# Three joints in blocks by halves of the tokens, and task matrices merged in two row groups between other products

## The reference

```
x = x + wide_attention(layernorm(x))             # 8 heads of 128, then @ Wout
x = x + merged_ffn(layernorm(x)):
    h = relu(x @ gate_w1.T + gate_b1);  g = mean over tokens(h @ gate_w2.T + gate_b2)    # 8 gates a batch
    mW1[b] = W1 + sum_e g[b,e] * TW1[e]          # 1024x256 for each of 16 batches
    mW2[b] = W2 + sum_e g[b,e] * TW2[e]
    out = gelu(x @ mW1[b].T + mb1) @ mW2[b].T + mb2
x = x + shared_key_attention(layernorm(x), ctx)  # L1_xattn
x = x + alibi_attention(layernorm(x))            # L1_attn
h = layernorm(x); h = h + rope_attention(rmsnorm(h)); mixture of experts       # L1_ffn
```

## Time and profile before

| | |
|---|---|
| median of 3 runs | 2373.8 us (2371.68 to 2376.3) |
| the profiled execution's own time | 2377.73 us |
| its span in the profile | 2375.9 us |
| mean granted clock of PE | 0.952 |
| busy: PE, DVE, ACT, POOL | 2179.1, 1314.4, 994.0, 332.1 us |

### The profile page before, as it was taken

How to read it: one execution, slowest core, us unless ns; L and a number is a source line. 1 busy time by engine, 2 the same in 40 slices (tenths; PEclk the granted TensorE clock), 3 DMA queues, 4 the chain that set the end, 5 groups by cost and what they waited for, 6 DMA issues and landing times. The chain is left out here.

```text
span 2375.9 us, 39783 instructions
## 1 busy us (share of the span) xinstructions
PE 2179.1 (92%) x15922; PEld 1507.1 (63%) x15922; DVE 1314.4 (55%) x2266; ACT 994.0 (42%) x1858; POOL 332.1 (14%) x366
## 2 busy tenths in 40 slices
PE   7999999999999977999998799978999998877796
PEld 4777777777777754555564677844555554545695
DVE  4556556656665634555553344347777772656554
ACT  1555555555555551343332011114666663515121
POOL 3322222222222200000000000032000000000231
PEclk9999999999999978999999899988999999898798
DMA  6877776777777521000000221123112111023312
GB/s 202 197 167 182 178 168 150 171 176 167 183 179 169 127 58 50 6 12 6 6 1 1 114 86 74 54 48 74 32 28 35 31 17 39 2 55 133 134 48 78
DMA packets 100570, 216.18 MB, mean 91 GB/s; under 512 B 58482, under 2 KB 66043, under 8 KB 94660
## 3 DMA queue, kind: packets, MB, share of 16 engines
q1 hardware_dynamic: 97652, 204.93, 34.9%
q0 software_dynamic: 2208, 6.03, 0.8%
q10 hardware_dynamic: 528, 2.69, 0.4%
HBM read 91.16 MB, written 15.20 MB: 45 GB/s over the span
## 5 line engine op out<-in xcount | busy, mean ns | idle before, releaser
L908 DVE TENSOR_REDUCE L_xattn_maxima<-L_xattn_scores 128x1 f32<-128x1024 f32 (+1 forms) x256 | 253.5, 990 | 249.2 <-PE L_xattn_scores L831 248.8
L975 ACT ACTIVATE L_xattn_probs_t<-L_xattn_turned 128x1024 f32<-128x1024 f32 (+1 forms) x256 | 220.8, 862 | 342.3 <-PE L_xattn_turned L843 342.3
L1812 DVE TENSOR_REDUCE shared_half_maxima<-shared_ring 128x1 f32<-128x578 f32 (+1 forms) x251 | 244.3, 990 | 88.3 <-PE shared_ring L1718 85.2
L1892 ACT ACTIVATE shared_exps<-shared_scores 128x512 f32<-128x512 f32 (+1 forms) x416 | 225.7, 594 | 122.5 <-PE shared_scores L1739 121.8
L987 ACT ACTIVATE L_xattn_probs<-L_xattn_scores,L_xattn_maxima 128x1024 f32<-128x1024 f32 (+1 forms) x256 | 235.6, 925 | 37.9 <-DVE L_xattn_maxima L911 37.9
L843 PEld LDWEIGHTS L_xattn_turned<-ident,L_xattn_probs 128*128 128x128 f32 x1664 | 198.0, 144 | 81.0 <-issue 48.1
L843 PE MATMUL L_xattn_turned<-ident,L_xattn_probs 128*128 128x128 f32 x1664 | 234.7, 281 | 14.1 <-ACT L_xattn_probs_t L975 12.0
L505 PE MATMUL L_xattn_projected<-L_xattn_wv,L_xattn_ctx 128*128 128x256 f32 x780 | 193.6, 390 | 0.0
L499 PE MATMUL L_xattn_projected<-L_xattn_ctx,L_xattn_wk 128*128 128x400 f32 x480 | 181.9, 501 | 0.0
L831 PE MATMUL L_xattn_scores<-L_xattn_k_stack,L_xattn_q_stack 128*128 128x512 f32 (+1 forms) x512 | 159.5, 393 | 22.2 <-ACT L_xattn_probs L987 11.1
L1739 PE MATMUL shared_scores<-shared_q,shared_k 128*128 128x512 f32 (+1 forms) x416 | 154.4, 449 | 0.1
(11 more groups left out here) (390 smaller groups left out, 3163.3 us busy)
## 6 DMA issues: line engine op xcount, KB each, us to landing
L_xattn_k_stack<-L_xattn_k_part SPq DMA_DIRECT2D x504, 200.2 KB, 4.3
L_xattn_ctx<-in_ctx_t SPq DMA_DIRECT2D x16, 1602.0 KB, 6.9
ffn_task<-in_ffn_task SPq DMA_DIRECT2D x16, 1024.0 KB, 6.7
experts_w_in<-in_expert_in SPq DMA_DIRECT2D x8, 1024.0 KB, 12.0
shared_k<-k_scratch SPq DMA_DIRECT2D x64, 100.1 KB, 3.3
L_xattn_q_stack<-q_scratch SPq DMA_DIRECT2D x128, 32.0 KB, 2.0
k_scratch<-L_xattn_shared_part SPq DMA_DIRECT2D x128, 32.0 KB, 1.7
shared_q<-q_scratch SPq DMA_DIRECT2D x64, 64.0 KB, 3.6
```

Source lines behind the costliest of these rows:

```text
L908: nc.vector.reduce_max(maxima[n % 2][:, half:half + 1], cols, axis=AX).then_inc(halves_maxed, 1)
L975: nc.scalar.activation(probs_t[:, t:t + m, p * P:(p + 1) * P], turned_tiles[:, 0:m, :], ACT.Copy).then_inc(turned_moved, 1)
L1812: nc.vector.reduce_max(half_maxima[:, n, half:half + 1], found[:, 0:HALF_STARTS[half + 1] - HALF_STARTS[half]], axis=AX).then_inc(ring_max ...
L1892: nc.scalar.activation(exps[n % 2][0:m, h * BANK:(h + 1) * BANK], scores[0:m, h, :], ACT.Exp, scale=SCALE).then_inc(exps_done, 1)
```

## The change

A new `joint_block` takes the place of `add_projection` and the `norm_block` behind it in the three joints. PE makes all output products, transposes half 0, runs `turn_after` tasks of half 0, transposes half 1 and runs the rest; tasks are now of one half each (`half_tasks`, and the rotary tasks ordered by half). DVE goes through one half wholly before the other: sums, statistics, root, normalising; its task moves come behind both. Keys are copied in two parts, and the attention waits for the part it reads.

In the feed-forward a merging product has 64 rows (one of two row groups) and 128 columns; a unit is four blocks times two groups, and fills both banks, one for each group, so that unit n waits for the move of unit n - 1. There are 4 units a matrix and tile, each moved by one DVE instruction of 1024 elements. The loop goes over the batches: at every second batch a merging unit, as long as there are any, then up for the batch, and downs of the tile before, lagging two batches. The memsets of the shared keys and queries go from the normalising block to the attention block.

```diff
+def joint_block(core, name, heads_t, chunks, weights, dst, dst_t, feature_scale=None, again=None, loads=(), task_loads=0, fills=(),
+                tasks=(), unit_banks=1, turn_after=2, copies=(), keys_copied=None, copies_after=(), pool_program=None):
...
+                def turn(half):
+                    for t in range(half * per_half, (half + 1) * per_half):
+                        pe.wait_ge(rows_ready, t + 1)
+                        for c in range(CHUNKS):
+                            last = nc.tensor.transpose(turned[:, HALVES * c + half, (t % per_half) * P:(t % per_half + 1) * P],
+                                                       last_rows[:, t, c * P:(c + 1) * P], core.ident[:])
+                    last.then_inc(turned_ready, 1)
+                def run_task(i):
+                    products, _, _, half = tasks[i]
+                    if i < slots:
+                        pe.wait_ge(row_added, per_half + unit_banks * (i + 1))
+                    else:
+                        on = tasks[i - slots][2]
+                        pe.wait_ge(moved[on], moved_count(on, i - slots + 1))
+                    pe.wait_ge(turned_moved, half + 1)
+                    for part, lhs_t, rhs, start, stop in products:
+                        last = nc.tensor.matmul(part(unit(i)), lhs_t, rhs, start=start, stop=stop)
+                    last.then_inc(products_ready, 1)
+                for t in range(TILES):
+                    if t >= 4:
+                        pe.wait_ge(row_added, t - 3)
+                    for k in range(chunks):
+                        last = nc.tensor.matmul(psum[:, t % 4, 0:DIM], heads_t[:, k, t * P:(t + 1) * P], weights[:, k, :],
+                                                start=k == 0, stop=k == chunks - 1)
+                    last.then_inc(row_done, 1)
+                turn(0)
+                pe.wait_ge(tasks_loaded, 16 * task_loads)
+                for i in range(turn_after):
+                    run_task(i)
+                turn(1)
+                for i in range(turn_after, len(tasks)):
+                    run_task(i)
...
+                for half in range(HALVES):
+                    rows = range(half * per_half, (half + 1) * per_half)
+                    variance = moments[:, half * per_half:(half + 1) * per_half, 1]
+                    for t in rows:
+                        dve.wait_ge(row_done, t + 1)
+                        nc.vector.tensor_tensor(x[:, t, :], psum[:, t % 4, 0:DIM], x[:, t, :], ALU.add).then_inc(row_added, 1)
+                        dve.wait_ge(row_added, t + 1)
+                        step(nc.vector.bn_stats(stats[:, t, :], x[:, t, :]))
...
+                    inverse_root(0, half)
+                    for t in rows:
+                        ins = nc.vector.tensor_scalar(dst[:, t, :], x[:, t, :], moments[:, t, 0:1],
+                                                      rstd[0][half][:, t % per_half:t % per_half + 1], ALU.subtract, ALU.mult)
...
+                for i in range(rounds):
+                    root(i, 0)
+                move_turned(0)
+                for i in range(rounds):
+                    root(i, 1)
+                act.wait_ge(tasks_loaded, 16 * task_loads)
+                run_moves(0, turn_after)
+                move_turned(1)
+                run_moves(turn_after, len(tasks))
...
-        add_projection(core, "wide_out", heads_t, WIDE_HEADS, wout, x)
...
+            joint_block(core, "ffn_joint", heads_t, WIDE_HEADS, wout, xn, xn_t_next,
...
+                        + [(gate_tiles["gb2_column"][:], dram["gate_b2"].unsqueeze(1))], task_loads=2, turn_after=CHUNKS,
+                        tasks=[task for half in range(HALVES) for task in half_tasks(
+                            core, gw1, xn_t_next, gate_t, gb1, True, half, ("act",) if half == 0 else ("act", "dve"))])
...
-MERGE_UNITS = 8
+MERGE_BLOCKS = 4
+MERGE_UNITS = 16 // MERGE_BLOCKS
+ROW_GROUPS = 2
+GROUP_ROWS = P // ROW_GROUPS
+GROUP_SPREAD = SPREAD // ROW_GROUPS
...
+        STEP_BATCHES = BATCH // (2 * MERGE_UNITS)
+        DOWN_LAG = 2
...
-                    if n >= 2:
-                        pe.wait_ge(merge_moved, n - 1)
+                    if n >= 1:
+                        pe.wait_ge(merge_moved, n)
                     for i, block_of in enumerate(blocks):
-                        last = nc.tensor.matmul(merging[:, n % 2, i * 2 * P:(i + 1) * 2 * P], block_of,
-                                                spread[:].rearrange("p b f -> p (b f)"), start=True, stop=True)
+                        for r in range(ROW_GROUPS):
+                            group = slice(r * GROUP_ROWS, (r + 1) * GROUP_ROWS)
+                            last = nc.tensor.matmul(merging[:, r, i * P:(i + 1) * P], block_of(group),
+                                                    spread[group].rearrange("p b f -> p (b f)"), start=True, stop=True)
                     last.then_inc(merge_done, 1)
...
+                def down(k, b):
+                    half, i = divmod(b, BATCH // HALVES)
+                    if b == 0:
+                        pe.wait_ge(merge_moved, second_units(k) + MERGE_UNITS)
+                    if i == 0:
+                        pe.wait_ge(hidden_ready, HALVES * k + half + 1)
+                    t, j = divmod(b, 2)
+                    last = nc.tensor.matmul(down_psum[j * SEQ:(j + 1) * SEQ, t // 2, (t % 2) * DIM:(t % 2 + 1) * DIM],
+                                            hidden_t[:, k, b * SEQ:(b + 1) * SEQ], merged_2[k % 2][:, b, :],
+                                            start=False, stop=k == HIDDEN_TILES - 1, skip_group_check=True)
...
-                    if m < HIDDEN_TILES - 1:
-                        merge_first(m + 1)
-                    up(m)
-                    merge_second(m)
-                    if m > 0:
-                        down(m - 1)
-                down(HIDDEN_TILES - 1)
+                    merges = [(merge_first, m + 1, j) for j in range(MERGE_UNITS)] if m < HIDDEN_TILES - 1 else []
+                    merges += [(merge_second, m, j) for j in range(MERGE_UNITS)]
+                    downs_done = 0
+                    for b in range(BATCH):
+                        if b % STEP_BATCHES == 0 and b // STEP_BATCHES < len(merges):
+                            merge, tile, j = merges[b // STEP_BATCHES]
+                            merge(tile, j)
+                        up(m, b)
+                        if m > 0:
+                            downs_due = max(b + 1 - DOWN_LAG, 0) * BATCH // (BATCH - DOWN_LAG)
+                            for i in range(downs_done, downs_due):
+                                down(m - 1, i)
+                            downs_done = downs_due
+                for b in range(BATCH):
+                    down(HIDDEN_TILES - 1, b)
...
+                            merged_unit(),
...
-                   fills=[(t[SPLIT_ROWS:].bitcast(F32), 0.0) for t in (*k, *q)],
...
-        add_projection(core, "shared_out", heads_t, CHUNKS, wo, x)
...
+                    if i == 1:
+                        pool.wait_ge(low_ready, len(query_units))
+                    for tile in (q[i], k[i]):
+                        nc.gpsimd.memset(tile[SPLIT_ROWS:].bitcast(F32), 0.0).then_inc(zeros_set, 1)
+                    pool.wait_ge(zeros_set, 2 * (i + 1))
...
+                    pe.wait_ge(keys_copied[u * HALVES // UNITS], 16 * GROUP_HEADS)
...
+        tasks = []
+        for half in range(HALVES):
+            tasks += half_tasks(core, wk, xn_t, k_t, bk, False, half, ("act",))
+            tasks += half_tasks(core, wq, xn_t, q_t, bq, False, half, ("act",) if half == 0 else ("dve",))
+            tasks += [task for task in value_tasks(nc, xn_t, wv, v) if task[3] == half]
+        per_half = len(tasks) // HALVES
...
+                    task_loads=5, tasks=tasks, turn_after=4, copies=key_block_copies(core, k_t), keys_copied=keys_copied,
+                    copies_after=(CHUNKS, per_half + CHUNKS), pool_program=make_bias)
...
+        tasks = [task for half in range(HALVES) for task in products if task[3] == half]
...
+        joint_block(core, "moe_joint", core.heads_t, CHUNKS, core.alibi_wo, h, hn_t, core.ln1, again=hn,
...
+                    task_loads=7, tasks=tasks, unit_banks=2, turn_after=2, copies=key_block_copies(core, k_t), keys_copied=keys_copied,
+                    copies_after=(CHUNKS, per_half + CHUNKS))
```

More of the change, by code:

```diff
@@ new lines, in half_products, with half_tasks, move_dve, move_act @@
+def half_products(weights, m, src_t, half, chunks=CHUNKS):
+    return [(lambda u: u[:, 0, :], weights[:, k, m * P:(m + 1) * P], src_t[:, k, half * BANK:(half + 1) * BANK],
+             k == 0, k == chunks - 1) for k in range(chunks)]
+def half_tasks(core, weights, src_t, dst, bias, relu, half, engines):
+    nc = core.nc
+    tasks = []
+    for m in range(CHUNKS):
+        def move_dve(unit, step, m=m):
+            out = dst[:, m, half * BANK:(half + 1) * BANK]
+            if relu:
```

(33 more changed lines are left out.)

288 lines of the change are left out of this document (190 added, 98 removed).

## The result

The changed kernel took 2383.2 us (median of 13 runs, 2380.1 to 2392.1), the kernel before 2372.8 (13 runs, 2368.9 to 2376.8): ratio 1.0047, 95% interval 1.0035 to 1.0059, so 0.5% or 10 to 11 us slower. The profiled execution has a span of 2381.5 us (run time 2383.3). The ratios of this document leave out executions more than 1.5% above the fastest of their kernel, which is one run of e9 (2361.7 us).

A forecast was written before the change was run, and what follows sets the result against it. It took TensorE (PE), busy 92% of the span, as the bound. Feed-forward with the clock +24 us and joints -15 gave +9 on a median of 2373.8, rounded to 2382; own range 2375 to 2395, wider range 2352 to 2440.

The forecast's parts named there:

- Part 1: Feed-forward merging in row groups: two groups run together, so a unit takes 0.88 us in 8 steps.
- Part 2: Feed-forward loop: 37 shape changes a tile and lone downs use up merging's gain; 26.3 us a tile against 26.0.
- The clock: Feed-forward opening at half clock, +16 us, next tile +8; with Part 1 and Part 2, +24 us.
- second term: Tile after the opening: the clock rises at its closing pair of downs or a little earlier, +8 us.
- Part 3: Three joints, each merging two blocks: -3.9, -5.0 and -2.8 us, with the shared norm's -3.4 a sum of -15.
- shared start: Shared norm: GpSimd's fills move behind the queries and no longer run beside the normalising, -3.4 us.
- (a): Rival: the clock rises inside the first hidden tile or is hardly lost, 2366 to 2374 us; chance 0.17.
- (b): Rival: full clock from the opening on and shape changes partly hidden, 2340 to 2358 us; chance 0.20.
- (c): Rival: half clock for three feed-forward tiles or more, 2400 to 2530 us; chance 0.17.
- (d): Rival: the merging's row groups don't run together, 2420 to 2440 us; chance 0.07.

The follow-up runs named there:

- e9: e8 with fewer fillers: 3 ahead of the gates, then 5, 1, 1, 0 behind the opening's units; 2337.7 us, ratio 0.9841.
- e3: The changed kernel with full-row merging products (128 rows, 256 columns) again, in the new order and units; 2407.4 us, ratio 1.0153.
- e4: The changed kernel with the downs issued two at a time, behind every second up; 2354.2 us, ratio 0.9922.
- e6: e5 with filler products on PE, results overwritten, in the wait for the bases and the opening's waits; 2369.7 us, ratio 1.0003.
- e11: e9 with 8 fillers behind the first merging unit instead of 5; 2330.7 us, ratio 0.9832.
- e2: The kernel before with the new feed-forward loop alone; 2399.7 us, ratio 1.0114.
- e5: The changed kernel with the 9-row bias products moved into the wait for the bases, ahead of the first merging unit; 2382.8 us, ratio 1.0040.
- e7: e6's fillers, but with the 9-row bias products left behind the opening's merging units; 2383.0 us, ratio 1.0026.
- e1: The changed kernel with the feed-forward block of the kernel before, so joints and moved fills alone; 2355.7 us, ratio 0.9941.
- e10: The changed kernel with its row-group units, but whole stages one after another as before; 2471.0 us, ratio 1.0409.
- e12: e9 with 7 fillers behind the opening's first unit and 2 behind each of the other three; 2327.8 us, ratio 0.9815.
- e8: e6 with the downs in pairs as in e4; 2340.8 us, ratio 0.9865.

## Why the prediction was right

It said 2382 (own range 2375 to 2395) and slower, giving slower a chance of 0.53 and the forecast itself 0.37; 2383.2 was measured, and its sum of +9 stands against +10.4. The measured terms lie close to the forecast ones, but one of them was not derived, and two were met closer in this execution than they repeat:

- **Part 1.** Forecast a unit in 8 steps of 0.107 to 0.112; measured 0.112, in pairs 0.007 apart. e3 shows what it is worth: 0.74 us a unit.
- **Part 2.** Unit 1.08 (1.09), up 0.58 (0.59), down 0.58 (0.58), step 3.40 (3.42), inner tile 26.3 (26.5), last tile 25.5 (25.7). So at full clock the merging's gain is spent on 37 changes of shape and lone downs. e4 shows this: with pairs and 23 changes a tile takes 4.5 us less.
- **The clock.** Opening 48 (48.7), next tile 34.3 (35.2); the whole block +24 (+26.7). e6 shows 20 us of it as the clock's, and e9 against e11 19.8 for the same loop. The size of the second term, +8 forecast and +8.7 measured, was luck in part. The place that the prediction names for the rise is the closing pair of downs, at the tile's end; by its own steps a whole tile at half clock is 48 us against 26.3, +22, and the forecast would have been some 2396. Only "or a little earlier" led to +8, without a working. In the profiles whose first tile ran at half clock the rise came amid lone downs (20 us into the second tile in the changed kernel and in e2, 14 in e5, 13 in e7) or pairs (30 in e4, 20 in e11). What they share is that the first tile, without downs, never raised it and the second did; why at these places is open.
- **Part 3.** First joint -3.9 (-3.7), second -5.0 (-4.8), third -2.8 (-3.0), shared start -3.4 (-3.3); sum -15, e1 measured -14. The second and third vary from execution to execution more than this agreement says: 33.2 to 37.7 us and 55.2 to 57.4 over the twelve profiles with the same joints, in the mean 3.5 and 2.1 us under the kernel before's profile. So the forecast -5.0 and -2.8 were 1.5 and 0.7 us too large, which the profiled execution hides. In e1's second joint PE waits 1.47 us for the normalising in the transposes, in the changed kernel's not. Why is open.
- **Rivals.** (a) and (b) needed an early clock: e6 is that case, and with 10 us of fillers on the path it equals the kernel before; without them the estimate is 2360, between the two. The sum in (b) gives 2337 to 2352, not the 2340 to 2358 that stands there. (c) didn't happen in 13 runs (2380 to 2392), though e10 shows a clock that falls in every tile. (d) is refuted by e3 and by the pairs of passes. Of the two rules of the Trainium skill, the drain at a change of tiling mode ("TensorEngine Tiling (Array Packing)", Key Properties) is what the loop pays for; e3's up without a change, 0.11 us shorter, agrees, though the weight load that nothing covers is in these 0.11 too. That a load goes by columns and not by rows ("TensorE: Matmul & The Clock Gate", LDWEIGHTS) may hold for one load, but sixteen 64-row loads didn't take as long as sixteen full ones: two loads in different row groups went side by side.

The prediction also leaves out that in the kernel before the clock had been up in the opening:

```profile
1359.40:1370.00 10.60, 9.89 (x36) 7.62 (x37) 5.40 (x9) 0.00 (x0) 0.00 (x0) 0.84 0.29 98
```

It rose there in the full-row merging and fell in the 9-row products L1437 at about 1370. The changed kernel's opening never gets that far, so e5, which moves these products, changes little.

What isn't settled: why the clock stays up in some runs of a kernel and falls in others behind the same waits; and how much of e12's remaining opening could be had by placing real work in the waits instead of fillers, which wasn't tried.

## What to carry to other kernels

When small products of different tile shapes are interleaved, each change costs 0.1 to 0.2 us here with its uncovered load, so count the changes first and put products of one shape together, above all those that fill two column halves as a pair. Halving PE's work in a stretch behind a wait can cost more than it saves: here the lighter first tile held the full clock when it had it, but at half clock didn't bring it up in 31 us. Read the granted clock of the stretch before, not only the busy share. Where a kernel's runs fall in two groups some 20 us apart, compare the clock by windows before believing a change.

## What the runs showed of the hardware

- The first tile of the same loop ran at full clock when it entered at full (profiles of e6, e8, e9, e12) and stayed at half for 31 us when it entered at half (changed kernel, e2, e4, e5). A tile of unchanged code thus costs 20.1 or 31.25 us, by the clock it starts with. The exception is e7's profile: it entered at full, right behind the 9-row products, and fell 2 us in.
- Runs of one kernel can fall in two groups by time and mean clock: 3 of 10 in e7's faster group, 3 of 6 in e9's, 4 of 6 in e11's, 10 of 12 in e6's. One profile of each kind (e9, e11) places the difference in the first two tiles of the feed-forward.
- 64 dense up passes of 64 columns ran 13.8 us at half clock without raising it (e10), and 7.2 us at full clock without losing it (kernel before).
- Two row groups loading and streaming side by side: pairs of 64*128 passes start 0.006 to 0.007 us apart, each pair 0.112 behind the last.
- A 128*64 down by itself and a pair of them in the two column halves take the same 0.58 us.
